# Two layernorms of a gated cross-attention block: applied by GpSimd in place of ScalarE

## The chip, the cores and the metric

One core of a Trainium2 chip. The metric is the device time of one execution in microseconds (us), the median over the runs. Engines by their names in the profile: PE and PEld are TensorE's matmuls and weight loads, DVE is VectorE, ACT is ScalarE, POOL is GpSimd, SP is SyncE.

## The reference

The input x is 16 tiles of 128 tokens by 256 features; each tile has a context of the same shape.

```python
def _layernorm(x, axis=-1, eps=1e-05):
    m = jnp.mean(x, axis=axis, keepdims=True)
    v = jnp.var(x, axis=axis, keepdims=True)
    return (x - m) / jnp.sqrt(v + eps)

x = x + jnp.tanh(g_xattn[0]) * _L0_xattn_ref(_layernorm(x, axis=-1), ctx_2048, Wq, Wk, Wv)
x = x + jnp.tanh(g_ffn[0]) * _L0_ffn_ref(_layernorm(x, axis=-1), wq_gate, s_gate, wq_up, s_up, wq_down, s_down)
```

`_L0_xattn_ref` is a cross-attention of 32 heads of width 8: queries from the first normalized x, keys and values from the context, an rms norm of each head's query and key, softmax, weighted sum. `_L0_ffn_ref` is a gated feed-forward layer of width 704 (silu of the gate times up, then down) on the second normalized x, with quantized integer weights. A layernorm ends as x times root plus offset, where root is 1/sqrt(v + eps) and offset is -m times root: one pair of numbers for each token, and a token is a partition.

## The kernel before

The 16 tiles go through in pairs. An iteration p (from -1 to 9) holds three stages of different tiles: it loads and projects the tiles 2p+2 and 2p+3, runs the attention of the tiles 2p-1 to 2p+1, and runs the feed-forward layer of pairs p-1 and p-2. Each engine has its own program, with the order of its work in an iteration written out by hand in a function `iteration(p)`; engines meet only at semaphores, and each engine works strictly in its order. `run` (line 302) unrolls the first iterations and the last ones and makes a hardware loop of p = 2 to 5. With e = 0 or 1 for the two halves of an iteration:

- TensorE (line 1420): `turn(p, e)` (line 1265) transposes the context and then the normalized tile `xn[:, e]` (L1273, L1277); it waits for `xn_ready`, count 2p+e+3, that is, for the first layernorm of tile 2p+e+2. `queries_keys(p, e)` (line 1290) and `values(p, e)` project (both L1286), `scores` (L1231) and `weigh` (L1250) are the attention, `out_rows` turns its result (L1319), `turn2(p)` (line 1341, L1351) transposes the second layernorm `x1n` of a pair, `chunk(p, j)` (L1371) are the six gate and up products and `down(p, e)` (L1396) the down product. Between the last matmul of `queries_keys(p, 0)` and `turn(p, 1)` TensorE has: scores, weigh, chunks 2 and 3, scores, weigh, chunk 4, weigh, scores, chunk 5.
- ScalarE (line 705): exponentials (L530), copies out of PSUM, squares of q and k (`square`, L572), tanh of the gate (L645), the upper part `h_hi` of the hidden values (`upper`, L656), and both layernorms: `normalize(p, e)` (line 585, L599) writes `xn[:, 1-e]` for tile b = 2p+e+3, and `normalize2(p, e)` (line 602, L611) writes `x1n[:, 1-e]` for tile b = 2p+e-1. So `turn(p, 1)` reads what `normalize(p, 0)` wrote, and `turn(p+1, 0)` reads what `normalize(p, 1)` wrote.
- VectorE (line 1104): statistics, the chain of small steps for the reciprocal roots (`roots`, L782 to L788; one chain serves the rms norms and the second layernorm), the upper half-precision part of q and k (`qk_upper`, L917), the copies that double it (`qk_double`, L929 to L931, after GpSimd's `split_qk`), the lower parts `xc_lo` (L894) and `x_lo` (L1028), the gates of the feed-forward layer (L983, L998). `up` of chunk j also waits until `h_lo` of chunk j-3 is done.
- GpSimd (line 477): in each iteration, in this order, `add_attention(p, 0)` (L443), `split_chunks` of chunks 0 and 1 (L434, the lower part `h_lo`), `qk_norm(p, 0)` (L466, q and k times their roots), `split_chunks` of chunk 2, `split_qk(p, 0)` (L426, the lower half-precision part), chunks 3, 4 and 5, `add_attention(p, 1)`, `qk_norm(p, 1)`, `split_qk(p, 1)`, and two `add_y` (L452, L454: scale and add the result of the feed-forward layer).

The roots of all 16 tiles for the first layernorm are made by VectorE in three batches early on (`x_bias_ready`), so `normalize` needs nothing new in the steady state. `normalize2` needs `x1_bias_ready`, which ends the root chain of the same half (`x1_offset`, L878).

Of the kernel before, what the change touches and what calls it, by code (L numbers as in the profile page):

```python
# [28 lines left out]
ALU = mybir.AluOpType  # L29
# [30 lines left out]
def build_program(nc, x, ctx, g_xattn, g_ffn, Wq, Wk, Wv, wq_gate, s_gate, wq_up, s_up, wq_down, s_down, out):  # L60
# [64 lines left out]
    with ExitStack() as stack:  # L125
# [188 lines left out]
        def has_tile(p, b):  # L314
            return 0 <= b < B if isinstance(p, int) else True
# [79 lines left out]
        @block.gpsimd  # L395
        def _(pool):
            nc.gpsimd.memset(ident[:], 0.0).then_inc(ident_zeroed, 1)
            pool.wait_ge(ident_zeroed, 1)
            nc.gpsimd.affine_select(out=ident[:], in_=ident[:], compare_op=ALU.not_equal, fill=1.0, base=0,
                                    pattern=[[-1, P]], channel_multiplier=1).then_inc(ident_ready, 1)  # L400

            nc.gpsimd.memset(v_blocks[:], 0.0).then_inc(v_zeroed, 1)
            pool.wait_ge(v_zeroed, 1)

            for e in range(2):
                v = v_blocks[:, e, 0:24 * BLOCK].rearrange("p (t c) -> p t c", c=3 * BLOCK)
                for i in range(3):
                    nc.gpsimd.memset(v[:, :, i * (BLOCK + SLOTW) + HD:i * (BLOCK + SLOTW) + HD + 1], 1.0)
                w = v_blocks[:, e, 24 * BLOCK:].rearrange("p (t c) -> p t c", c=2 * BLOCK)
                for i in range(2):  # L410
                    nc.gpsimd.memset(w[:, :, i * (BLOCK + SLOTW) + HD:i * (BLOCK + SLOTW) + HD + 1], 1.0)

                last = nc.gpsimd.memset(w[:, :, 3 * SLOTW - 1:3 * SLOTW], 1.0)
            last.then_inc(v_ready_ones, 1)

            nc.gpsimd.memset(y_sb[:, 0, :], 0.0).then_inc(result_ready, 1)
            nc.gpsimd.memset(y_sb[:, 1, :], 0.0).then_inc(result_ready, 1)

            def split_qk(p, e):

                b = 2 * p + e
                if not has_tile(p, b + 2):
                    return
                pool.wait_ge(qk_hi_ready, b + 3)
                pool.wait_ge(unit_ready, b + 3)
                nc.gpsimd.tensor_tensor(qk_parts[:, :, 1, :], qk_unit[:], qk_parts[:, :, 0, :],  # L426
                                        ALU.subtract).then_inc(qk_lo_ready, 1)

            def split_hidden(p, q, j):

                n = NJ * (p - q) + j
                pool.wait_ge(h_hi_ready, n + 1)
                r = rows(j)
                nc.gpsimd.tensor_tensor(h_lo[0:r, j, :], hidden[0:r, j % 3, :], h_hi[0:r, j, :].bitcast(F32),  # L434
                                        ALU.subtract).then_inc(h_lo_ready, 1)

            def add_attention(p, e):

                b = 2 * p + e - 1
                if has_tile(p, b):  # L440
                    k, n = use(p, f"out{e}")
                    pool.wait_ge(drained[k], n)
                    nc.gpsimd.tensor_tensor(tile_of(b), tile_of(b), attn[:], ALU.add).then_inc(x1_ready, 1)  # L443

            def add_y(p, e):

                if isinstance(p, int) and p == PAIRS + 1:
                    return
                done = 2 * (p - 2) + e
                k, n = use(p, f"y{e}")  # L450
                pool.wait_ge(drained[k], n)
                nc.gpsimd.tensor_tensor(y_sb[:, e, :], y_sb[:, e, :], down_scale[:], ALU.mult).then_inc(y_scaled, 1)  # L452
                pool.wait_ge(y_scaled, done + 1)
                nc.gpsimd.tensor_tensor(tile_of(done), tile_of(done), y_sb[:, e, :], ALU.add).then_inc(result_ready, 1)  # L454

            def qk_norm(p, e):

                b = 2 * p + e
                if not has_tile(p, b + 2):
                    return  # L460
                pool.wait_ge(root_steps, (ROOT_STEPS + 1) * (b + 3))
                k, m = use(p, f"qk{e}")
                pool.wait_ge(drained[k], m)
                if since(b, -1):
                    pool.wait_ge(qk_lo_ready, b + 2)
                nc.gpsimd.tensor_tensor(qk_unit[:], qk_raw[:], root_y[:, 0:2 * H].unsqueeze(2).to_broadcast([P, 2 * H, HD]),  # L466
                                        ALU.mult).then_inc(unit_ready, 1)

            def real(p, task):
                return here(p, task) and not (isinstance(p, int) and p == 0)  # L470

            def split_chunks(p, q, chunks):
                if real(p, f"ffn{chunks[0]}"):
                    for j in chunks:
                        split_hidden(p, q, j)

            def iteration(p):
                add_attention(p, 0)
                split_chunks(p - 1, 1, (0, 1))
                qk_norm(p, 0)  # L480
                split_chunks(p, 2, (2,))
                split_qk(p, 0)
                split_chunks(p, 2, (3, 4, 5))
                add_attention(p, 1)
                qk_norm(p, 1)
                split_qk(p, 1)
                if real(p, "y0"):
                    add_y(p, 0)
                    add_y(p, 1)

            run(pool, iteration)

        @block.scalar
        def _(act):
# [87 lines left out]
                        act.wait_ge(qk_hi_ready, b + 2)  # L582
                    nc.scalar.copy(qk_raw[:].rearrange("p h d -> p (h d)"), bank[k][:]).then_inc(drained[k], 1)

            def normalize(p, e):

                b = 2 * p + e + 3
                if not has_tile(p, b):
                    return
                if isinstance(b, int):  # L590
                    batch = 1 + [b < last for first, last in BATCHES].index(True)
                    act.wait_ge(x_bias_ready, batch)
                    one = slice(b, b + 1)
                else:
                    one = bass.ds(b, 1)
                if since(b, 2):
                    k, m = use(p, "turn0") if e else use(p - 1, "turn1")
                    act.wait_ge(filled[k], m)
                nc.scalar.activation(xn[:, 1 - e, :], tile_of(b), ACT.Identity, bias=x_bias[:, one],  # L599
                                     scale=x_root[1][:, one]).then_inc(xn_ready, 1)  # L600

            def normalize2(p, e):

                b = 2 * p + e - 1
                if not has_tile(p, b):
                    return
                act.wait_ge(x1_bias_ready, b + 1)
                if since(b, 2):
                    k, m = use(p if e else p - 1, "turn2")
                    act.wait_ge(filled[k], m)  # L610
                nc.scalar.activation(x1n[:, 1 - e, :], tile_of(b), ACT.Identity, bias=x1_bias[:], scale=root_y[:, 2 * H:]).then_inc(x1n_ready, 1)  # L611

            def drain_y(p, e):

                task = f"y{e}"
# [68 lines left out]
            def begin(p):  # L684
# [10 lines left out]

                exp_octet(p, 0, 1)
                drain_v(p, 0)
                if not first:
                    normalize(p, 0)
                upper(p - 1, 1, 0)  # L700
                if isinstance(p, int) and p == PAIRS + 1:
                    tanh_chunk(p, 2, 2)
# [2 lines left out]
            def iteration(p):  # L705
# [3 lines left out]

                exp_octet(p, 0, 2)  # L710
                copy_qk(p, 0)
                if first:
                    normalize(p, 0)
                if not (isinstance(p, int) and p == PAIRS + 1):
                    tanh_chunk(p, 2, 2)
                tanh_chunk(p, 2, 3)

                exp_octet(p, 0, 3)
                upper(p, 2, 2)
                if isinstance(p, int) and p == PAIRS - 1:  # L720
                    normalize2(p, 0)
                tanh_chunk(p, 2, 4)
                if ending(p):
                    upper(p, 2, 3)
# [1 line left out]
                drain_pv(p, 1)  # L726
                exp_octet(p, 1, 0)
                tanh_chunk(p, 2, 5)
                if isinstance(p, int) and p == PAIRS:
                    normalize2(p, 0)  # L730
                turn_hi(p, 1)

                exp_octet(p, 1, 1)
                if not ending(p):
                    upper(p, 2, 3)
                    normalize2(p, 0)
                upper(p, 2, 4)
                drain_v(p, 1)
                upper(p, 2, 5)
                if first:  # L740
                    convert_gate_up()
                    square(p, 1)
                    copy_qk(p, 1)
                    convert_down()
                    normalize(p, 1)
                else:
                    normalize(p, 1)
                    square(p, 1)
                    copy_qk(p, 1)

# [2 lines left out]
                drain_y(p, 0)  # L753

                exp_octet(p, 1, 3)
                if not (isinstance(p, int) and p == 0):
                    normalize2(p, 1)
                drain_y(p, 1)
                tanh_chunk(p, 1, 0)
                tanh_chunk(p, 1, 1)  # L760
                if isinstance(p, int) and p == 0:
                    normalize2(p, 1)
                begin(p + 1)

            upper_weight(0)
            normalize(-2, 1)
            upper_weight(1)
            begin(FIRST)
            run(act, iteration)
# [726 lines left out]
```

## Time and profile before

| | us |
|---|---|
| median of 3 runs | 257.71 |
| lowest, highest | 256.37, 260.33 |
| span of the profiled execution, first to last instruction | 254.6 |
| PE busy in the span | 217.0 (85%) |
| DVE busy | 189.1 (74%) |
| ACT busy | 176.9 (69%) |
| POOL busy | 107.6 (42%) |

The runs give whole device times; the profiled execution has only its span. The median of the runs is 3.1 us above that span, so a predicted span is compared with the runs after adding 3.1 us. A busy share says how much of the span an engine worked, not whether the end waited for it. Times in the rows are counted from the start of the span.

### The profile page before, as it was taken

The numbers are of one execution on the slowest core, as the hardware profiler recorded it, in microseconds if no ns is written. First come the engines' busy times: TensorE is split into PE (matmuls) and PEld (weight loads), VectorE is DVE, ScalarE is ACT, GpSimd is POOL, SyncE is SP. The second block draws the span as 40 slices with busy tenths as digits, with TensorE's granted clock in tenths as the row PEclk, the third lists the DMA queues.
The fourth block names the chain that finished last, engine by engine and source line by source line (L and its number), as shares of the span: only waits on it lengthen the run. The fifth ranks groups of instructions, "written<-read, shape, count | busy, mean of one in ns | idle before, by whom it ended". The sixth has DMA issues, their size and how long they took to land.

```text
span 254.6 us, 7326 instructions
## 1 busy us (share of the span) xinstructions
PE 217.0 (85%) x2592; PEld 175.6 (69%) x2592; DVE 189.1 (74%) x583; ACT 176.9 (69%) x338; POOL 107.6 (42%) x145
## 2 busy tenths in 40 slices
PE   1664878949869999999999999999999998983974
PEld 1553746727558888778878887888788776773873
DVE  4587999872878778786878687968796887667163
ACT  3358593746877896879688958895889588455261
POOL 5012303031314382737184728463835473454442
PEclk9999996777999999999999999999999999999799
DMA  6798631405061524141323223322315041000001
GB/s 176 220 351 209 72 58 21 86 5 107 0 106 35 71 23 86 36 108 33 70 47 97 42 61 61 83 56 51 76 50 64 21 82 48 21 24 0 21 21 41
DMA packets 45128, 18.08 MB, mean 71 GB/s; under 512 B 36401, under 2 KB 44849, under 8 KB 45105
## 3 DMA queue, kind: packets, MB, share of 16 engines
q1 hardware_dynamic: 45104, 17.77, 32.9%
q8 instruction: 14, 0.23, 0.4%
q14 instruction: 10, 0.07, 0.1%
HBM read 7.28 MB, written 2.10 MB: 37 GB/s over the span
## 4 chain that ended last, share of the span: by engine, by line
PE 62%; DVE 17%; issue 8%; ACT 7%; DMA 2%; POOL 2%; SPq 1%; DVEq 0%; ACTq 0%
PE bank L1371 16%; PE bank L1286 14%; PE pv_ps L1250 10%; PE bank L1396 9%; PE score_ps L1231 5%; DVE silu L983 2%; PE bank L1319 2%; ACT probs L530 2%; DVE hidden L998 2%; ACT tanh_g L645 2%; DMA w_raw<-L_xattn_Wv_dram 2%; DVE xc_lo L894 1%; PE bank L1277 1%; PE bank L1273 1%; PE bank L1351 1%
## 5 line engine op out<-in xcount | busy, mean ns | idle before, releaser
L530 ACT ACTIVATE probs<-score_ps 128x1024 f32<-128x1024 f32 x64 | 66.0, 1033 | 2.7 <-PE score_ps L1231 2.7
L466 POOL TENSOR_TENSOR qk_unit<-qk_raw,root_y 128x512 f32<-128x512 f32 x16 | 17.4, 1084 | 86.0 <-DVE root_y L788 86.0
L1371 PE MATMUL bank<-x_hi,gu_hi 128*128 128x256 f32 (+1 forms) x192 | 49.8, 296 | 4.0 <-DVE hidden L998 2.0
L1250 PE MATMUL pv_ps<-probs,v_blocks 128*32 128x128 f32 x1024 | 43.0, 287 | 6.3 <-issue 3.8
L1371 PE MATMUL bank<-x_lo,gu_hi 128*128 128x256 f32 (+1 forms) x192 | 47.1, 281 | 0.0
L434 POOL TENSOR_TENSOR h_lo<-hidden,h_hi 128x256 fp32r<-128x256 f32 (+1 forms) x48 | 36.7, 772 | 21.1 <-ACT h_hi L656 20.3
L1371 PEld LDWEIGHTS bank<-x_hi,gu_hi 128*128 128x128 f32 (+1 forms) x192 | 34.3, 179 | 8.8 <-issue 4.6
L1250 PEld LDWEIGHTS pv_ps<-probs,v_blocks 128*32 128x32 f32 x1024 | 25.1, 112 | 15.8 <-issue 6.6
L1286 PE MATMUL bank<-w_hi,xc_hi 128*128 128x256 f32 x96 | 31.7, 330 | 3.8 <-DVE xc_lo L894 3.8
L1371 PEld LDWEIGHTS bank<-x_lo,gu_hi 128*128 128x128 f32 (+1 forms) x192 | 34.5, 180 | 0.0
L645 ACT ACTIVATE tanh_g<-bank,half_gate 128x256 f32<-128x256 f32 (+1 forms) x48 | 22.7, 474 | 14.8 <-PE bank L1371 13.4
L983 DVE SCALAR_TENSOR_TENSOR silu<-tanh_g,bank 128x256 f32<-128x256 f32 (+1 forms) x48 | 19.9, 415 | 13.5 <-ACT tanh_g L645 13.4
L1231 PE MATMUL score_ps<-q_stack,k_stack 32*128 32x128 f16 x512 | 26.0, 223 | 4.5 <-DMA k_stack<-qk_parts 4.5
L1286 PE MATMUL bank<-w_hi,xc_lo 128*128 128x256 f32 x96 | 29.1, 303 | 0.0
L1286 PE MATMUL bank<-w_lo,xc_hi 128*128 128x256 f32 x96 | 29.1, 303 | 0.0
L1286 PEld LDWEIGHTS bank<-w_hi,xc_hi 128*128 128x128 f32 x96 | 20.4, 213 | 8.7 <-DVE xc_lo L894 5.1
L1231 PEld LDWEIGHTS score_ps<-q_stack,k_stack 32*128 32x128 f16 x512 | 14.8, 95 | 15.5 <-issue 7.9
L1396 PE MATMUL bank<-dn_hi,h_hi 128*128 128x256 f32 x84 | 25.2, 327 | 0.0
L998 DVE SCALAR_TENSOR_TENSOR hidden<-silu,scales,bank 128x256 f32<-128x256 f32 (+1 forms) x48 | 22.9, 478 | 2.4
L426 POOL TENSOR_TENSOR qk_parts<-qk_unit,qk_parts 128x512 f16<-128x512 f32 x16 | 18.6, 1162 | 8.8 <-DVE qk_parts L917 8.8
L1396 PE MATMUL bank<-dn_hi,h_lo 128*128 128x256 f32 x84 | 22.1, 290 | 0.0
L656 ACT CAST h_hi<-hidden 128x256 fp32r<-128x256 f32 (+1 forms) x48 | 18.7, 405 | 3.8 <-DVE hidden L998 3.6
(108 smaller groups left out, 438.0 us busy)
## 6 DMA issues: line engine op xcount, KB each, us to landing
ctx_sb<-ctx_dram SPq DMA_DIRECT2D x16, 128.0 KB, 2.6
out_dram<-x_all SPq DMA_DIRECT2D x16, 128.0 KB, 1.8
x_all<-x_dram SPq DMA_DIRECT2D x1, 1536.0 KB, 11.3
dn_int<-L_ffn_wq_down_dram SPq DMA_DIRECT2D x1, 704.0 KB, 7.6
gu_int<-L_ffn_wq_gate_dram SPq DMA_DIRECT2D x1, 640.0 KB, 4.6
gu_int<-L_ffn_wq_up_dram SPq DMA_DIRECT2D x1, 640.0 KB, 5.6
x_all<-x_dram SPq DMA_DIRECT2D x1, 384.0 KB, 4.5
w_raw<-L_xattn_Wq_dram SPq DMA_DIRECT2D x1, 256.0 KB, 2.7
```

The lines of the kernel that those rows point to most:

```text
L426: nc.gpsimd.tensor_tensor(qk_parts[:, :, 1, :], qk_unit[:], qk_parts[:, :, 0, :], ALU.subtract).then_inc(qk_lo_ready, 1)
L434: nc.gpsimd.tensor_tensor(h_lo[0:r, j, :], hidden[0:r, j % 3, :], h_hi[0:r, j, :].bitcast(F32), ALU.subtract).then_inc(h_lo_ready, 1)
L530: nc.scalar.activation(probs[:, t % 2, :], score_ps[t % 2][:].rearrange("p h n -> p (h n)"), ACT.Exp, scale=float(HD) ** 0.5 / UNIT ** 2). ...
L645: nc.scalar.activation(tanh_g[0:r, j % 2, :], bank[k][0:r, 0:TOK], ACT.Tanh, scale=half_gate[0:r, j:j + 1]).then_inc(tanh_g_ready, 1)
L656: nc.scalar.copy(h_hi[0:r, j, :], hidden[0:r, j % 3, :]).then_inc(h_hi_ready, 1)
L983: nc.vector.scalar_tensor_tensor(out=silu2[0:r, j % 2, :], in0=tanh_g[0:r, j % 2, :], scalar=1.0, in1=bank[k][0:r, 0:TOK], op0=ALU.add, op ...
L998: nc.vector.scalar_tensor_tensor(out=hidden[0:r, j % 3, :], in0=silu2[0:r, j % 2, :], scalar=scales[0:r, 2, j:j + 1], in1=bank[k][0:r, TOK ...
L1231: last = nc.tensor.matmul(score_ps[t % 2][:, s, :], k_stack[of, e, g, :], q_stack[of, e, g, :], start=True, stop=True, tile_position=(BLOC ...
L1250: last = nc.tensor.matmul(pv_ps[BLOCK * quadrant:BLOCK * (quadrant + 1), region * P:(region + 1) * P], v_blocks[:, e, h * BLOCK:(h + 1) * ...
L1286: last = nc.tensor.matmul(dst, a[:, tile, KC * source + c, :], w[:, c, column * D:(column + 1) * D], start=(n == 1), stop=(n == 3 * KC))
L1371: last = nc.tensor.matmul(bank[k][0:r, a * TOK:(a + 1) * TOK], w[:, j, a, c, 0:r], xx[:, c, :], start=(n == 1), stop=(n == (4 if wide_weig ...
L1396: last = nc.tensor.matmul(bank[k][:, 0:D], hh[0:r, j, e * P:(e + 1) * P], w[0:r, j, :], start=(n == 1), stop=(n == (4 if wide_weights else ...
```

## The change

`normalize` and `normalize2` leave ScalarE's program and are made by GpSimd as one `tensor_scalar` with two per-partition scalars (times root, plus offset). Their places in GpSimd's iteration are new, and GpSimd's program is unrolled over all iterations in place of `run`.

```diff
+            def normalize(p, e):
+                b = 2 * p + e + 3
+                if not has_tile(p, b):
+                    return
+                pool.wait_ge(x_bias_ready, 1 + [b < last for first, last in BATCHES].index(True))
+                if b >= 2:
+                    k, m = use(p, "turn0") if e else use(p - 1, "turn1")
+                    pool.wait_ge(filled[k], m)
+                nc.gpsimd.tensor_scalar(xn[:, 1 - e, :], x_all[:, b, :], x_root[1][:, b:b + 1], x_bias[:, b:b + 1],
+                                        ALU.mult, ALU.add).then_inc(xn_ready, 1)
+
+            def normalize2(p, e):
+                b = 2 * p + e - 1
+                if not has_tile(p, b):
+                    return
+                pool.wait_ge(x1_bias_ready, b + 1)
+                if b >= 2:
+                    k, m = use(p if e else p - 1, "turn2")
+                    pool.wait_ge(filled[k], m)
+                nc.gpsimd.tensor_scalar(x1n[:, 1 - e, :], x_all[:, b, :], root_y[:, 2 * H:], x1_bias[:],
+                                        ALU.mult, ALU.add).then_inc(x1n_ready, 1)
...
             def iteration(p):
                 add_attention(p, 0)
                 split_chunks(p - 1, 1, (0, 1))
+                if p == FIRST:
+                    normalize(p, 0)
                 qk_norm(p, 0)
+                normalize2(p, 0)
                 split_chunks(p, 2, (2,))
                 split_qk(p, 0)
+                if p != FIRST:
+                    normalize(p, 0)
                 split_chunks(p, 2, (3, 4, 5))
                 add_attention(p, 1)
                 qk_norm(p, 1)
+                normalize2(p, 1)
                 split_qk(p, 1)
+                normalize(p, 1)
                 if real(p, "y0"):
                     add_y(p, 0)
                     add_y(p, 1)
 
-            run(pool, iteration)
+            normalize(-2, 1)
+            for p in range(FIRST, PAIRS + 2):
+                iteration(p)
...
-                nc.scalar.activation(xn[:, 1 - e, :], tile_of(b), ACT.Identity, bias=x_bias[:, one],
-                                     scale=x_root[1][:, one]).then_inc(xn_ready, 1)
...
-                nc.scalar.activation(x1n[:, 1 - e, :], tile_of(b), ACT.Identity, bias=x1_bias[:], scale=root_y[:, 2 * H:]).then_inc(x1n_ready, 1)
```

All calls of the two functions in ScalarE's program go.

## Rows read from the trace of the kernel before

**Rows 1.** the page: span and busy time of each engine

```profile
span 254.6 us, 7326 instructions
...
PE 217.0 (85%) x2592; PEld 175.6 (69%) x2592; DVE 189.1 (74%) x583; ACT 176.9 (69%) x338; POOL 107.6 (42%) x145
```

**Rows 2.** the page: the chain that ended last, by engine

```profile
PE 62%; DVE 17%; issue 8%; ACT 7%; DMA 2%; POOL 2%; SPq 1%; DVEq 0%; ACTq 0%
```

**Rows 3.** busy us by engine in one stretch, then clock, DMA, GB/s

```profile
117.00:142.00 25.00, 24.70 (x327) 20.07 (x318) 19.85 (x58) 20.27 (x40) 13.56 (x16) 1.00 0.29 63
```

**Rows 4.** TensorE's waits: us in total, times, longest

```profile
PE bank L1286 <- DVE xc_lo L894: 3.8, 6, 1.5
```

**Rows 5.** timeline, PE: start us, us, line, what, idle before

```profile
128.84 0.38 PE L1277 MATMUL bank<-ident,xn 128*128 128x128 f32 x2
...
140.64 0.38 PE L1277 MATMUL bank<-ident,xn 128*128 128x128 f32 x2
```

**Rows 6.** groups by form, ACT: busy us, mean ns, idle before

```profile
L611 ACT ACTIVATE x1n<-x_all,x_bias,root_y 128x256 f32 x8 | 4.9, 607 | 4.5 <-DVE x_bias L878 4.5
L599 ACT ACTIVATE xn<-x_all,x_bias,x_root_y 128x256 f32 x8 | 4.8, 605 | 0.0
```

**Rows 7.** groups by form, POOL

```profile
L443 POOL TENSOR_TENSOR x_all<-x_all,attn 128x256 f32 x8 | 5.9, 735 | 4.7 <-DVE attn L957 4.7
...
L416 POOL MEMSET y_sb<- 128x256 f32 x1 | 0.3, 312 | 0.0
L399 POOL TENSOR_SCALAR_AFFINE_SELECT ident<-ident 128x128 f32<-128x128 f32 x1 | 0.3, 294 | 0.2 <-POOL ident L397 0.2
```

**Rows 8.** timeline, POOL, one steady iteration

```profile
125.45 1.08 POOL L466 TENSOR_TENSOR qk_unit<-qk_raw,root_y 128x512 f32<-128x512 f32 x1 [4.53 <-DVE root_y L788]
127.16 1.17 POOL L426 TENSOR_TENSOR qk_parts<-qk_unit,qk_parts 128x512 f16<-128x512 f32 x1 [0.62 <-DVE qk_parts L917]
...
138.29 1.10 POOL L466 TENSOR_TENSOR qk_unit<-qk_raw,root_y 128x512 f32<-128x512 f32 x1 [3.77 <-DVE root_y L788]
139.35 1.19 POOL L434 TENSOR_TENSOR h_lo<-hidden,h_hi 128x256 fp32r<-128x256 f32 x1
140.50 1.16 POOL L426 TENSOR_TENSOR qk_parts<-qk_unit,qk_parts 128x512 f16<-128x512 f32 x1
```

**Rows 9.** timeline, DVE, the same stretch

```profile
125.46 1.62 DVE L917 TENSOR_TENSOR qk_parts<-qk_raw,root_y 128x512 f16<-128x512 f32 x1
...
137.82 0.22 DVE L788 SCALAR_TENSOR_TENSOR root_y<-root_p,root_y 128x65 f32<-128x65 f32 x1
...
138.80 1.13 DVE L917 TENSOR_TENSOR qk_parts<-qk_raw,root_y 128x512 f16<-128x512 f32 x1
```

**Rows 10.** timeline, PE, the first iterations: transposes of xn

```profile
27.23 0.64 PE L1277 MATMUL bank<-ident,xn 128*128 128x128 f32 x2
...
40.23 0.40 PE L1277 MATMUL bank<-ident,xn 128*128 128x128 f32 x2
...
67.42 0.38 PE L1277 MATMUL bank<-ident,xn 128*128 128x128 f32 x2
```

**Rows 11.** timeline, POOL, the first iterations

```profile
27.25 1.16 POOL L426 TENSOR_TENSOR qk_parts<-qk_unit,qk_parts 128x512 f16<-128x512 f32 x1 [0.63 <-DVE qk_parts L917]
...
40.57 1.16 POOL L426 TENSOR_TENSOR qk_parts<-qk_unit,qk_parts 128x512 f16<-128x512 f32 x1 [1.90 <-DVE qk_parts L917]
...
69.00 1.17 POOL L426 TENSOR_TENSOR qk_parts<-qk_unit,qk_parts 128x512 f16<-128x512 f32 x1 [0.63 <-DVE qk_parts L917]
```

**Rows 12.** PE in stretches: busy us, granted clock, DMA, GB/s

```profile
36.90:40.30 3.40, 1.12 (x15) 1.00 0.00 0
40.30:47.20 6.90, 6.90 (x49) 0.51 0.49 87
...
234.90:238.30 3.40, 3.40 (x16) 0.52 0.00 0
```

**Rows 13.** timeline, DVE, near the end

```profile
231.76 0.63 DVE L788 SCALAR_TENSOR_TENSOR root_y<-root_p,root_y 128x65 f32<-128x65 f32 x1
```

More of the change, by code:

```diff
@@ L583, in copy_qk @@
                     nc.scalar.copy(qk_raw[:].rearrange("p h d -> p (h d)"), bank[k][:]).then_inc(drained[k], 1)
[L585 to L598, printed above, removed]
-                nc.scalar.activation(xn[:, 1 - e, :], tile_of(b), ACT.Identity, bias=x_bias[:, one],
-                                     scale=x_root[1][:, one]).then_inc(xn_ready, 1)
[L602 to L610, printed above, removed]
-                nc.scalar.activation(x1n[:, 1 - e, :], tile_of(b), ACT.Identity, bias=x1_bias[:], scale=root_y[:, 2 * H:]).then_inc(x1n_ready, 1)
             def drain_y(p, e):
@@ L697, in begin @@
                 drain_v(p, 0)
-                if not first:
-                    normalize(p, 0)
                 upper(p - 1, 1, 0)
@@ L711, in iteration @@
                 copy_qk(p, 0)
-                if first:
-                    normalize(p, 0)
                 if not (isinstance(p, int) and p == PAIRS + 1):
@@ L719, in iteration @@
                 upper(p, 2, 2)
-                if isinstance(p, int) and p == PAIRS - 1:
-                    normalize2(p, 0)
                 tanh_chunk(p, 2, 4)
@@ L728, in iteration @@
                 tanh_chunk(p, 2, 5)
-                if isinstance(p, int) and p == PAIRS:
-                    normalize2(p, 0)
                 turn_hi(p, 1)
@@ L735, in iteration @@
                     upper(p, 2, 3)
-                    normalize2(p, 0)
                 upper(p, 2, 4)
@@ L744, in iteration @@
                     convert_down()
-                    normalize(p, 1)
                 else:
-                    normalize(p, 1)
                     square(p, 1)
@@ L755, in iteration @@
                 exp_octet(p, 1, 3)
-                if not (isinstance(p, int) and p == 0):
-                    normalize2(p, 1)
                 drain_y(p, 1)
@@ L760, in iteration @@
                 tanh_chunk(p, 1, 1)
-                if isinstance(p, int) and p == 0:
-                    normalize2(p, 1)
                 begin(p + 1)
             upper_weight(0)
-            normalize(-2, 1)
             upper_weight(1)
```

## The prediction

> **What bounds the kernel now.** I read the page first: the span is 254.6 us, PE is busy for 85% of it, ACT for 69%, POOL for 42% [rows 1]. Busy shares are averages, so next comes the chain that ended last: 62% of it is PE, 7% ACT [rows 2]. Then one steady stretch of 25 us, which is one iteration: PE is busy for 24.7 of 25.0 us, ACT for 20.3, POOL for 13.6 [rows 3]. So in the steady state TensorE is the bound, and no engine that is relieved can give back more than some 0.3 us an iteration; TensorE's own waits say the same, the nearest steady one being six waits on VectorE's `xc_lo` [rows 4]. Of the two layernorms on ScalarE no wait of TensorE in the steady state is seen. ScalarE spends 32 x 0.605 = 19.4 us on them (16 tiles, two norms; each of the two rows shown has a twin of 8) [rows 6], but it has nearly 5 us idle an iteration already.
>
> The question is then not what ScalarE gains but when the results are ready on GpSimd. The timelines of one iteration on PE, POOL and DVE answer that.
>
> **The price of one layernorm on GpSimd.** The trace has no such instruction, so bounds: below, GpSimd's write-only memset of 128x256, 0.31 us; above, `split_qk`, a two-input operation of twice the width, 1.16 us [rows 7, 8]. Nearer: a one-input operation of half the width takes 0.29 us, the two-input one of the same width 0.735 us [rows 7]. With 0.1 us fixed, the one-input row doubled gives about 0.49. There are two scalars to fetch, so I take 0.60, between 0.49 and 0.735, and 0.56 from start to start for back-to-back instructions.
>
> The Trainium skill (GPSIMD Engine Reference, section 3.1) gives 1.8 cycles an element at 1.2 GHz as the best case of its loops: by that an estimate of 0.38 us before dispatch. No row here shows it; by it alone the sum below would be about 5 us less.
>
> **The first layernorm for `turn(p, 1)`: the main cost.** `turn(p, 1)` transposes what `normalize(p, 0)` wrote. In the trace TensorE does that at 140.64 [rows 5]; ScalarE had the tile ready 8 us earlier. In the new order `normalize(p, 0)` stands behind `qk_norm(p, 0)`, `normalize2(p, 0)`, chunk 2's `h_lo` and `split_qk(p, 0)`. `qk_norm(p, 0)` can't start before the roots of the same iteration are done: the last root step starts at 137.82 and ends at 138.04, `qk_norm` starts at 138.29 [rows 8, 9]. Before, `split_qk` ended at 140.50 + 1.16 = 141.66, already 1.0 us after TensorE wants the tile. `normalize2` ahead of it adds 0.56, `normalize` itself 0.56, the semaphore 0.05: ready at 142.83. TensorE stands still for 142.83 - 140.64 = 2.2 us. All that TensorE has queued waits with it: scores, `out_rows`, weigh, `values`, `queries_keys(p, 1)`, `turn2`, `down`. Nothing of it gives the time back, because the next such chain starts only at the next `queries_keys(p+1, 0)`. Iterations 2 to 6 pay it: 5 x 2.2 = 11.0 us.
>
> The port between VectorE and GpSimd is in these numbers: `qk_upper` takes 1.13 us when it starts 0.59 us before GpSimd's `qk_norm` ends, and 1.62 us when it starts with it; each time it ends about 0.54 us after `qk_norm` does [rows 8, 9]. So the GpSimd instruction behind `qk_norm` waits 0.5 us in its turn (chunk 2 took 1.19 us). Before the change chunk 2 carried that wait, after it `normalize2` does; it is paid once either way.
>
> The Trainium skill (SBUF — State Buffer, "Who interferes with whom") says that a VectorE instruction with two SBUF inputs and a GpSimd instruction that reads block each other wholly, whoever comes second; these two durations agree. By a rule of shared bandwidth the sum would be the same to 0.2 us an iteration.
>
> **The first layernorm for `turn(p+1, 0)`.** `qk_norm(p, 1)` ended at 126.53, `qk_upper` at 127.08. `normalize2(p, 1)` starts behind `qk_norm`, is held until 127.08 and ends at 127.5 (0.16 of its 0.60 being start-up), `split_qk` ends at 128.66, `normalize(p, 1)` at 129.25, seen by TensorE at 129.30; it wanted the tile at 128.84 [rows 5, 8, 9]. That is 0.45 us, in iterations 1 to 5: 2.3 us. The two `add_y` behind it come some 0.9 us later, which GpSimd's idle time before the next `qk_norm` (3.77 us, [rows 8]) hides.
>
> **First iterations.** The layernorm of tile 1 is made as soon as its offset is there, as before, 0.1 us later by GpSimd's slower wake-up. `turn(0, 0)` was at 27.23; `normalize(-1, 1)` now follows a `split_qk` that ends at 28.41, so ready at 29.05: 1.8 us late, of which I take 1.4, since the following stretch hangs on VectorE (bounds 0 and 1.8). `turn(0, 1)` was at 40.23, the `split_qk` ends at 41.73, so 42.34: 2.1 us. `turn(1, 1)` was at 67.42; `split_qk` ended at 70.17, with `normalize2` ahead 70.5, ready at 71.1: 3.6 us, since this iteration has few chunks between projection and turn [rows 10, 11]. Together 7.2 us. The tile for `turn(1, 0)` has time to spare.
>
> **The end.** The last `normalize2` now blocks GpSimd until its roots are there, so the `h_lo` instructions no longer collide with VectorE's root steps: a step that took 0.63 us [rows 13] takes 0.22 elsewhere [rows 9], and one more is alike. That gives back 0.9 us, of which 0.4 goes again as `h_lo` of chunk 2 comes late for `up` of chunk 5. With an earlier `x_lo`, I take -0.7, bounds -1.0 and +0.5. Unrolling GpSimd's program I cost at nothing: its instructions start back to back in the loop already.
>
> **The clock.** In the stretch 36.9 to 40.3 PE was busy for only 1.12 us; then the granted clock is 0.51 for 6.9 us, that is the 1.2 GHz level, and after 234.9, behind a long idle stretch, 0.52 for 3.4 us [rows 12]. A stall of 2.2 us with light work about it comes near the first case. One such fall costs 3.4/2 = 1.7 us to 6.9/2 = 3.4 us. I take two falls (iteration 1, with its long stall, and one of the five others) at 2.5 us: 5 us. Bounds: none, and one for every stall.
>
> **Sum.** 254.6 + 11.0 + 2.3 + 0.1 + 7.2 - 0.7 + 5 = 279.5 us of span, 282.6 as a run (+3.1). I say 282.
>
> **Rivals.**
> 1. The same waits, the clock never falls: 282 - 5 = 277. For it: the steady stretch is at 1.00 throughout, and a stall is only a twelfth of an iteration. Chance 0.20.
> 2. The clock falls after nearly every stall: seven falls at 2.5 us in place of two, 277 + 17.5 = 295. For it: the fall after 40.3, behind an idle time of about the same length. Against: next to these stalls there are dense products, there were few. Chance 0.12. The Trainium skill (TensorE: Matmul & The Clock Gate, "HAM oscillation") describes kernels in which TensorE's wait in each turn of a loop brings the lower clock each time; the two falls here agree that idle time is what brings it.
> 3. GpSimd's layernorm costs as much as its slowest rows, 1.1 us in place of 0.6. Each such 0.1 us counts about 25 times 0.1 (two in each of the waits above, one in the first ones): +12.5, 290 with the clock as forecast. Against: it has one input. Chance 0.08. At 0.31 us the waits of `turn(p+1, 0)` vanish and the sum is about 7 us less, 275; that lies in the forecast's own range.
> 4. Not slower. The place is the path from `queries_keys(p, 0)` to `split_qk(p, 0)` on ScalarE and VectorE: if ScalarE without its 1.2 us a half iteration ran squares and tanh so much earlier that the roots came 2.2 us sooner, the tile would be there in time, and only the 0.3 us waits and the end would be left: 257.7 - 6 x 0.3 - 0.7 = 255. It decides from 2.2 us. Against: the root steps run back to back on VectorE, and ScalarE took the squares as soon as TensorE was done. Chance 0.10, most of it for a dependency that I read wrongly.
>
> **Chances.** Forecast 0.50, its own range 272 to 291; rivals 0.20, 0.12, 0.08, 0.10. The range 266 to 296 takes in rivals 1 to 3 and a cheap layernorm without a fall of the clock. Less than 2% is about what a measurement of this kernel can't tell from no change, that is 252.6 to 262.9: slower by more 0.90, within it 0.06, faster 0.04.
>
> **What would show it.** Right: TensorE waits at L1277 for GpSimd's `xn` in nearly every iteration, about 2.2 us for e = 1 and under 0.7 for e = 0; the period grows from 25.0 to 27.7 us; the layernorm takes near 0.6 us; ScalarE's busy time falls by 19 us and the time still rises; stretches at the 1.2 GHz level stand behind some of the stalls. Wrong: no wait at L1277; a layernorm over 1 us; the growth in VectorE's copies (a port that both want) in place of TensorE's wait; or a period that is unchanged.

## The result and the profile after

| | before | after |
|---|---|---|
| median, us | 258.94 (4 runs) | 285.62 (4 runs, 284.9 to 287.41) |
| span of the profiled execution, us | 254.6 | 283.3 |
| PE busy, us | 217.0 | 231.4 |
| mean granted clock of the profiled execution | 0.966 | 0.886 |

The ratio is 1.1116, 95% interval 1.1025 to 1.1207: the change makes the kernel 11% slower. (The median of before is over one run more than in the first table.) Ratios and intervals, here and below, leave out the runs in which the same kernel was in a slower state and use its other runs alone, so they are not the quotients of the medians in the table.

The page of the changed kernel, busy time by engine and the chain that ended last:

```profile
span 283.3 us, 7217 instructions
...
PE 231.4 (82%) x2592; PEld 185.4 (65%) x2592; DVE 185.8 (66%) x583; ACT 163.2 (58%) x306; POOL 128.0 (45%) x177
...
PE 54%; issue 15%; POOL 12%; DVE 11%; ACT 4%; DMA 1%; SPq 1%; DVEq 0%; ACTq 0%; POOLq 0%
```

Against [rows 1, 2]: ACT works 13.7 us less and POOL 20.4 us more, with 32 instructions moved. The forecast had 19.4 us for ACT, which is 32 durations added up [rows 6]; but in the trace of before these instructions overlap their neighbours (the layernorm at 132.13 lasts 0.60 us, the next instruction starts at 132.63), and busy time counts an overlap once. PE works 14.4 us more on the same 2592 matmuls, and it is idle for 283.3 - 231.4 = 51.9 us in place of 37.6. So the 28.7 us of the span are two nearly equal halves: 14.3 us in which TensorE waits, and 14.4 us in which the same work takes longer. Not all of the 14.4 is the change's: this execution also has a stretch at the lower clock from about 19 to 35 us, which the trace of before hasn't, and two kernels below without the late tile whose executions have it too show PE busy for 218.3 and 218.8 us, 1.3 to 1.8 above before. By stages (from one transpose of `xn` to another): 12.3 of the 28.7 us are lost by `turn(2, 1)` (102.80 in place of 90.50), 15.5 in the four steady iterations behind it, 0.9 after the last turn. POOL has risen in the chain from 2% to 12%. Lines of the code have moved: L1277 (transposes of `xn`) is now L1266, L1286 is L1275, L466 is L490, L426 is L450, and the two layernorms are L428 and L440.

Who TensorE waited for (us in total, times, longest):

```profile
PE bank L1266 <- POOL xn L428: 18.9, 10, 3.5
...
PE bank L1275 <- DVE xc_lo L883: 3.3, 2, 1.8
PE bank L1340 <- DVE hidden L987: 3.2, 1, 3.2
...
PE bank L1360 <- DVE x_lo L1017: 1.2, 1, 1.2
```

The first line is new and is the largest of all: 18.9 us in ten waits for GpSimd's first layernorm. Of the others that on `xc_lo` is a little smaller, in two waits where [rows 4] had six, that for the last turn is 3.2 us in place of 3.8, that on `x_lo` 1.2 in place of 2.0; none is more than 0.5 us larger than before.

GpSimd in one iteration, and the price of the layernorm by groups (busy us, mean ns):

```profile
126.53 1.08 POOL L490 TENSOR_TENSOR qk_unit<-qk_raw,root_y 128x512 f32<-128x512 f32 x1 [3.66 <-DVE root_y L777]
127.73 0.56 POOL L440 TENSOR_SCALAR x1n<-x_all,root_y,x_bias 128x256 f32<-128x256 f32 x1
128.25 1.16 POOL L458 TENSOR_TENSOR h_lo<-hidden,h_hi 128x256 fp32r<-128x256 f32 x1
129.38 1.15 POOL L450 TENSOR_TENSOR qk_parts<-qk_unit,qk_parts 128x512 f16<-128x512 f32 x1
130.51 0.55 POOL L428 TENSOR_SCALAR xn<-x_all,x_root_y,x_bias 128x256 f32<-128x256 f32 x1
...
142.69 1.07 POOL L490 TENSOR_TENSOR qk_unit<-qk_raw,root_y 128x512 f32<-128x512 f32 x1 [4.49 <-DVE root_y L777]
143.75 0.99 POOL L440 TENSOR_SCALAR x1n<-x_all,root_y,x_bias 128x256 f32<-128x256 f32 x1
144.71 1.17 POOL L450 TENSOR_TENSOR qk_parts<-qk_unit,qk_parts 128x512 f16<-128x512 f32 x1
145.86 0.56 POOL L428 TENSOR_SCALAR xn<-x_all,x_root_y,x_bias 128x256 f32<-128x256 f32 x1
```

```profile
L440 POOL TENSOR_SCALAR x1n<-x_all,root_y,x_bias 128x256 f32<-128x256 f32 x16 | 12.4, 773 | 9.9 <-DVE x_bias L867 9.3
...
L428 POOL TENSOR_SCALAR xn<-x_all,x_root_y,x_bias 128x256 f32<-128x256 f32 x16 | 9.3, 582 | 10.5 <-DVE x_bias L810 10.5
```

The order is the one written out in the change, and it answers to [rows 8]: `qk_norm` at 126.53, then `normalize2`, chunk 2, `split_qk`, and only at 130.51 the layernorm that TensorE needs. It takes 0.55 us and ends at 131.06. The group of `x1n` has a mean of 0.77 us since in the second half of an iteration it is held (0.99 us at 143.75, where VectorE's `qk_upper` runs from 142.85 to 144.32), and in the first half it isn't (0.56 us at 127.73, ahead of `qk_upper` at 127.94).

TensorE at the same places, and the granted clock about the stall (columns of the second fence: stretch, length, PE busy, instructions, clock, DMA, GB/s):

```profile
102.80 0.44 PE L1266 MATMUL bank<-ident,xn 128*128 128x128 f32 x2 [1.90 <-POOL xn L428]
...
131.12 0.69 PE L1266 MATMUL bank<-ident,xn 128*128 128x128 f32 x2 [1.91 <-POOL xn L428]
...
147.18 0.38 PE L1266 MATMUL bank<-ident,xn 128*128 128x128 f32 x2
...
160.69 0.44 PE L1266 MATMUL bank<-ident,xn 128*128 128x128 f32 x2 [1.92 <-POOL xn L428]
...
188.86 0.69 PE L1266 MATMUL bank<-ident,xn 128*128 128x128 f32 x2 [1.92 <-POOL xn L428]
...
218.50 0.44 PE L1266 MATMUL bank<-ident,xn 128*128 128x128 f32 x2 [1.83 <-POOL xn L428]
```

```profile
97.50:101.00 3.50, 3.41 (x46) 1.00 0.00 0
101.00:104.50 3.50, 1.70 (x17) 0.85 0.00 0
104.50:108.00 3.50, 3.50 (x32) 0.66 0.96 75
108.00:111.50 3.50, 3.50 (x44) 1.00 0.55 119
...
129.00:132.50 3.50, 1.59 (x13) 0.75 0.00 0
132.50:136.00 3.50, 3.50 (x28) 0.50 0.35 67
136.00:139.50 3.50, 3.50 (x40) 0.77 0.56 121
139.50:143.00 3.50, 3.50 (x43) 1.00 0.00 0
```

Each of the turns with e = 1 waits 1.8 to 1.9 us [rows 5: no idle time there before]; the turn with e = 0 at 147.18 doesn't wait. After each stall the clock is at its 1.2 GHz level for a while, about 3.3 us behind the stall at 102.80 and about 6.5 us behind the one at 131.12; the iterations are alternately 28.3 and 29.6 us long (102.80, 131.12, 160.69, 188.86, 218.50), against 25.0 before.

### The profile page after: what moved, and what is told of

Read it like the earlier page. It is cut to its first block, busy times and chain, and to the rows that moved or that the text cites. A ratio compares the mean times of both kernels' runs of the same rounds, so it can differ in the third digit from the quotient of the medians.

```text
span 283.3 us, 7217 instructions
## 1 busy us (share of the span) xinstructions
PE 231.4 (82%) x2592; PEld 185.4 (65%) x2592; DVE 185.8 (66%) x583; ACT 163.2 (58%) x306; POOL 128.0 (45%) x177
## 4 chain that ended last, share of the span: by engine, by line
PE 54%; issue 15%; POOL 12%; DVE 11%; ACT 4%; DMA 1%; SPq 1%; DVEq 0%; ACTq 0%; POOLq 0%
PE bank L1275 15%; PE bank L1385 10%; PE pv_ps L1239 8%; PE bank L1360 7%; PE score_ps L1220 5%; POOL qk_parts L450 4%; POOL qk_unit L490 3%; PE bank L1308 3%; PE bank L1266 2%; POOL xn L428 2%; POOL h_lo L458 2%; ACT probs L563 2%; DMA w_raw<-L_xattn_Wv_dram 1%; PE bank L1340 1%; DVE hidden L987 1%
## 5 line engine op out<-in xcount | busy, mean ns | idle before, releaser
L490 POOL TENSOR_TENSOR qk_unit<-qk_raw,root_y 128x512 f32<-128x512 f32 x16 | 17.2, 1076 | 77.2 <-DVE root_y L777 77.2
L1239 PE MATMUL pv_ps<-probs,v_blocks 128*32 128x128 f32 x1024 | 45.3, 299 | 6.8 <-issue 4.3
L1275 PE MATMUL bank<-w_hi,xc_hi 128*128 128x256 f32 x96 | 35.6, 371 | 3.4 <-DVE xc_lo L883 3.3
L1239 PEld LDWEIGHTS pv_ps<-probs,v_blocks 128*32 128x32 f32 x1024 | 26.1, 116 | 17.0 <-issue 8.0
L650 ACT ACTIVATE tanh_g<-bank,half_gate 128x256 f32<-128x256 f32 (+1 forms) x48 | 22.7, 473 | 19.9 <-PE bank L1360 17.8
L1275 PE MATMUL bank<-w_lo,xc_hi 128*128 128x256 f32 x96 | 32.4, 337 | 0.0
L1275 PE MATMUL bank<-w_hi,xc_lo 128*128 128x256 f32 x96 | 32.1, 334 | 0.0
L972 DVE SCALAR_TENSOR_TENSOR silu<-tanh_g,bank 128x256 f32<-128x256 f32 (+1 forms) x48 | 19.9, 414 | 16.0 <-ACT tanh_g L650 15.9
L1275 PEld LDWEIGHTS bank<-w_hi,xc_hi 128*128 128x128 f32 x96 | 24.3, 254 | 8.9 <-issue 4.6
L956 DVE BATCH_NORM_STATS2 x_stats<-x_all 128x6 f32<-128x256 f32 (+1 forms) x16 | 6.8, 427 | 27.5 <-POOL x_all L467 27.5
L1275 PEld LDWEIGHTS bank<-w_lo,xc_hi 128*128 128x128 f32 x96 | 24.4, 254 | 0.0
L1275 PEld LDWEIGHTS bank<-w_hi,xc_lo 128*128 128x128 f32 x96 | 23.8, 248 | 0.0
```

The source lines that it names most:

```text
L650: nc.scalar.activation(tanh_g[0:r, j % 2, :], bank[k][0:r, 0:TOK], ACT.Tanh, scale=half_gate[0:r, j:j + 1]).then_inc(tanh_g_ready, 1)
L972: nc.vector.scalar_tensor_tensor(out=silu2[0:r, j % 2, :], in0=tanh_g[0:r, j % 2, :], scalar=1.0, in1=bank[k][0:r, 0:TOK], op0=ALU.add, op ...
L1239: last = nc.tensor.matmul(pv_ps[BLOCK * quadrant:BLOCK * (quadrant + 1), region * P:(region + 1) * P], v_blocks[:, e, h * BLOCK:(h + 1) * ...
L1275: last = nc.tensor.matmul(dst, a[:, tile, KC * source + c, :], w[:, c, column * D:(column + 1) * D], start=(n == 1), stop=(n == 3 * KC))
```

## The experiments

Theory: the time is lost at one place, `turn(p, 1)`, since `normalize(p, 0)` stands behind `split_qk(p, 0)` in GpSimd's order; a direct wait and the lower clock that each wait brings. Rival: it is the load, 32 more instructions on an engine that shares a port with VectorE. The median of before, over the runs that the ratios use, was 258.35 us for the first four experiments, 258.59 us for the next three and 258.84 us for the last two (over all runs 259.32, 259.22 and 259.23 us). The recorded ratios and the quotients of these medians differ by up to 0.005, so a difference of half a per cent is settled by neither.

**One layernorm in another place.**

```diff
-                if p == FIRST:
-                    normalize(p, 0)
+                normalize(p, 0)
                 qk_norm(p, 0)
...
                 split_qk(p, 0)
-                if p != FIRST:
-                    normalize(p, 0)
```

> Both layernorms stay on GpSimd, only normalize(p, 0) moves ahead of qk_norm(p, 0). Place theory (TensorE waits because that layernorm stands behind split_qk): the e=1 waits at the xn transposes, 1.9 us in each steady iteration and 3.5 us in iteration 1, go, and with them the stretches at the 1.2 GHz level behind them; TensorE's wait on xn falls from 18.9 us to 2 to 4 us (the first turns and e=0), the period from 28.9 to about 25.5 us, the time to 258 to 264 us. Load theory (GpSimd's longer program and the port that it shares with VectorE cost the time): the time stays above 275 us, since the same 32 instructions run on the same engine.

Measured: 258.26 us, ratio 1.0013 (0.9974 to 1.0052). Its waits and a steady stretch (busy us of PE, PEld, DVE, ACT, POOL, then clock):

```profile
PE bank L1263 <- POOL xn L428: 3.1, 2, 1.7
```

```profile
117.00:142.00 25.00, 24.91 (x325) 20.14 (x325) 19.95 (x59) 18.59 (x36) 16.33 (x21) 1.00 0.29 63
```

The wait for `xn` is 3.1 us in two, both in the first iterations. The steady clock is 1.00, the period 24.8 us. POOL is busy for 16.3 of 25 us where it had 13.6 [rows 3], and this costs nothing: the load theory falls here. The move of one call gives back the whole loss, 27 us.

**The other half early too.** In addition, `normalize(p, 1)` ahead of `qk_norm(p, 1)`:

```diff
+                normalize(p, 1)
                 qk_norm(p, 1)
                 normalize2(p, 1)
                 split_qk(p, 1)
-                normalize(p, 1)
```

> As the run before, and normalize(p, 1) ahead of qk_norm(p, 1) too, so no first layernorm stands behind a split_qk. Place theory: no wait on xn is left but that of tile 1 (1.2 us, there before as well); the time is that of the kernel before within 1%, or a little below by the end (255 to 260 us). Load theory: no better than the run before, above 275 us.

Measured: 258.82 us, ratio 0.9991 (0.9945 to 1.0036). Left is one wait of 2.6 us for `xn`, that of tile 1, which a kernel with ScalarE's layernorm shows at 2.6 us too in one of its executions (the unrolled kernel below). Nothing more is gained by it than by the first move; the steady period is 25.0 us.

**Is it the clock?** The changed kernel, with TensorE given something to do where it stands still:

```diff
                 k = claim(p, f"turn{e}")
+                if e == 1 and since(p, 2):
+                    for _ in range(14):
+                        nc.tensor.matmul(bank[k][:, 0:D], dn_hi[:, 0, 0:P], dn_hi[:, 0, :], start=True, stop=True)
                 pe.wait_ge(ctx_loaded[e], 16 * (p + 2))
```

> The changed kernel, with 14 extra matmuls of 128x256 (about 1.7 us at 2.4 GHz, their result overwritten) put into TensorE's stall ahead of turn(p, 1) for p of 2 and more. They fill a wait of 1.9 us. Clock theory (half of the lost time is the lower clock that each stall brings): the clock stays at the 2.4 GHz level in the steady state, mean granted clock 0.94 or more against 0.886, period near 27.2 us, time 8 to 11 us below the changed kernel, 274 to 278 us, though TensorE does more. Wait theory (the stalls alone cost, the low clock is hidden by other waits): the time stays within 2 us of 285.6 or rises.

Measured: 277.12 us, ratio 1.0678 (1.0614 to 1.0742); that is 8.5 us below the changed kernel, with 70 matmuls more. Two stretches of it and its wait (PE busy, instructions, clock):

```profile
120.00:148.00 28.00, 27.73 (x344) 1.00 0.30 64
148.00:176.00 28.00, 27.70 (x361) 1.00 0.30 64
```

```profile
PE bank L1269 <- POOL xn L428: 10.8, 10, 3.5
```

With the stall filled the clock stays at 1.00 in the steady state and the iteration takes 26.8 us. (The profiled execution is the fastest of the four, with a mean clock of 0.947; the other three, without a trace of their own, have 0.907 to 0.913 and are 1.2 to 2.0 us longer.) The order of GpSimd is the same and the tile is as late as before (0.3 us of wait are left beside the filling). So of the 3.9 us that an iteration of the changed kernel is longer (28.9 on the mean against 25.0), 1.8 are the late tile and 2.1 are the lower clock that the standstill brings. The wait theory (stalls alone) falls.

**Unrolling alone.** The kernel before with one edit:

```diff
-            run(pool, iteration)
+            for p in range(FIRST, PAIRS + 2):
+                iteration(p)
```

> The kernel before with nothing changed but GpSimd's program unrolled. No layernorm is moved. Theory that unrolling is free: ratio 1.00 within 0.5%. Rival: in the changed kernel qk_norm starts 0.17 us sooner after the last root step and takes the port ahead of the one-column offset (0.93 us in place of 0.15), which puts qk_upper 0.4 us later in each half (p, 0); by it this run shows the same 0.9 us offset instruction in the steady iterations, and the time is 0 to 2 us above before, more likely near 0 as TensorE does not wait there.

Measured: 258.02 us, ratio 0.9939 (0.9899 to 0.9979), a little faster, where I had expected nothing or a loss. The medians are nearer to each other, 258.02 against 258.35 us, 0.999, so the size of the gain isn't settled. The offset instruction does take 0.92 us, as the rival says (VectorE and GpSimd in the first half of an iteration):

```profile
140.18 0.22 DVE L789 SCALAR_TENSOR_TENSOR root_y<-root_p,root_y 128x65 f32<-128x65 f32 x1
...
140.65 0.92 DVE L879 SCALAR_TENSOR_TENSOR x_bias<-x_mean_var,root_y 128x1 f32<-128x1 f32 x1
...
141.89 0.91 DVE L918 TENSOR_TENSOR qk_parts<-qk_raw,root_y 128x512 f16<-128x512 f32 x1
```

```profile
140.48 1.08 POOL L466 TENSOR_TENSOR qk_unit<-qk_raw,root_y 128x512 f32<-128x512 f32 x1 [3.20 <-DVE root_y L789]
```

`qk_norm` now starts 0.30 us after the last root step's start, before 0.47 [rows 8, 9], and starts ahead of the offset, which then ends with it. The time isn't longer for it. What the trace shows as gained is at another place, where VectorE's copies meet GpSimd's two `add_y`:

```profile
132.06 0.38 DVE L930 COPY qk_parts<-qk_parts 128x256 f32<-128x256 f32 x1
132.37 0.75 DVE L931 COPY qk_parts<-qk_parts 128x128 f32<-128x128 f32 x1
133.04 0.21 DVE L932 COPY qk_parts<-qk_parts 128x128 f32<-128x128 f32 x1
...
133.46 0.62 DVE L895 TENSOR_TENSOR xc_lo<-bank,xc_hi 128x512 fp32r<-128x512 f32 x1
```

```profile
130.75 0.73 POOL L452 TENSOR_TENSOR y_sb<-y_sb,down_scale 128x256 f32<-128x256 f32 x1
131.56 0.73 POOL L454 TENSOR_TENSOR x_all<-x_all,y_sb 128x256 f32<-128x256 f32 x1
132.25 0.78 POOL L452 TENSOR_TENSOR y_sb<-y_sb,down_scale 128x256 f32<-128x256 f32 x1
```

GpSimd's instructions follow each other 0.81 us apart where the loop had 0.92 (128.28 and 129.20 in the trace of before), so the copies (L930 to L932) meet other gaps: 0.38, 0.75 and 0.21 us, against 0.77, 0.75 and 0.21 before. `xc_lo` comes earlier, the 0.3 us wait that TensorE had for it in each steady iteration is gone (two such waits are left, where [rows 4] had six), and the period is 24.8 us. That is some 1.2 us over five iterations. It is a matter of which instructions happen to meet, not of unrolling as such: the run with both halves early and that with the second layernorm alone (below) are unrolled too, and keep six such waits and 25.0 us.

**One norm at a time.** First the first layernorm alone on GpSimd, in its places of the change (the calls of `normalize2` stay in ScalarE's program, those of `normalize` go):

> Only the first layernorm moves to GpSimd, in the places of the change; the second stays on ScalarE. Place theory: the tile for turn(p, 1) still stands behind split_qk, but without the 0.56 us of normalize2 ahead of it: steady wait at the xn transposes 1.9 - 0.56 = 1.3 us in place of 1.9, and the lower clock behind at least some of the stalls; time 268 to 280 us. Load theory: half the load, so half of the 27 us: 272 us, with the growth spread and no wait at the xn transposes that explains it.

Measured: 279.53 us, ratio 1.0846 (1.0764 to 1.0928). The steady wait is 1.5 us (1.3 expected): `normalize2` ahead of it is worth 0.4 us of lateness, and the rest of the chain alone is enough for the stall.

```profile
PE bank L1301 <- POOL xn L428: 16.4, 10, 3.2
```

Then the second layernorm alone on GpSimd, the first on ScalarE:

> Only the second layernorm moves to GpSimd, in the places of the change; the first stays on ScalarE. Place theory: nothing of TensorE's waits for it in the steady state, so 256 to 261 us, ratio within 1% of before, by 0 to 1 us better at the end. Load theory: half the load, half the loss, 272 us.

Measured: 258.85 us, ratio 0.9992 (0.9937 to 1.0047). The same count of instructions moved costs 20 us in the one case and nothing in the other, so it isn't the load.

**How early is early enough?** Both on GpSimd, `normalize(p, 0)` right behind `qk_norm(p, 0)`:

```diff
                 qk_norm(p, 0)
+                if p != FIRST:
+                    normalize(p, 0)
                 normalize2(p, 0)
...
                 split_qk(p, 0)
-                if p != FIRST:
-                    normalize(p, 0)
```

> Both on GpSimd, normalize(p, 0) right behind qk_norm(p, 0), ahead of normalize2, chunk 2 and split_qk. It tests the sum of the chain: the last root step ends, qk_norm ends some 1.4 us later, the layernorm takes 0.55 us (0.5 more if it is held by the port), so the tile is ready 2.0 to 2.5 us after the last root step, and TensorE wants it 2.6 us after. Place theory: no steady wait or one under 0.2 us, 258 to 263 us. Rival (anything behind qk_norm is too late, as TensorE needs the tile before the roots are done): waits of 1 us or more, 268 us and up.

Measured: 263.57 us, ratio 1.0193 (1.0113 to 1.0272), at the upper edge of what was expected. GpSimd and TensorE in the steady state:

```profile
121.38 1.08 POOL L490 TENSOR_TENSOR qk_unit<-qk_raw,root_y 128x512 f32<-128x512 f32 x1 [3.61 <-DVE root_y L777]
122.44 0.56 POOL L428 TENSOR_SCALAR xn<-x_all,x_root_y,x_bias 128x256 f32<-128x256 f32 x1
```

```profile
123.90 0.38 PE L1266 MATMUL bank<-ident,xn 128*128 128x128 f32 x2
```

The tile is ready at 123.00 and TensorE takes it at 123.90, without a wait: 0.9 us to spare, and the period is 24.7 us. What is left of the loss is in the first iterations, which have fewer chunks between projection and turn: four waits, 7.2 us in all. One of them is tile 1's, 2.6 us in this execution as in two others that lose nothing by it; the other three (1.7, 1.8 and 1.1 us) make 4.6. My expectation had left these out.

**Does a version beat both?** The version with `normalize(p, 0)` early, and `normalize(-1, 1)` early as well:

> The version with normalize(p, 0) early, and normalize(-1, 1) early too, so that no turn of the first iterations waits for a split_qk either. Place theory: against the version with normalize(p, 0) early the 1.7 us wait at the xn transposes of turn(0, 0) goes; of it 0.5 to 1.4 us are saved; ratio to before 0.990 to 0.998. Rival (the first iterations hang on VectorE and the clock, not on that wait): no difference from the version with normalize(p, 0) early, ratio 0.996 to 1.003.

Measured: 258.13 us, ratio 0.993 (0.9902 to 0.9959). The wait at `turn(0, 0)` is gone; of the waits for `xn` only tile 1's is left, 1.2 us. By the interval it is the first version with both layernorms on GpSimd that is faster than the kernel before, by 0.7%; by the medians (258.13 against 258.84 us) it is 0.3%, and the version without this last move has 258.26 us. So neither a gain over the kernel before nor one over that version is settled, and its interval overlaps that of the plain unrolled kernel: that the layernorms' move brings any gain isn't shown.

The kernel before, unrolled, with only the three last second layernorms on GpSimd:

> The kernel before with GpSimd's program unrolled, and of the layernorms only the last three second ones (p of 7 and 8) on GpSimd. In the last iterations the two steps of VectorE's root chain that GpSimd's h_lo held up should run at 0.22 us, TensorE's longest wait for the last turn2 falls from 3.8 to 3.2 us, and the steady state keeps the period of the unrolled kernel, 24.8 us. Expected ratio 0.988 to 0.994, below the unrolled kernel by 0.5 us. Rival (the saved 0.6 us goes again on the last chunks): same as the unrolled kernel, 0.994.

Measured: 257.51 us, ratio 0.9963 (0.992 to 1.0005). TensorE's longest wait for the last turn is 3.2 us in place of 3.8, as expected, but the ratio lies above the expected 0.988 to 0.994 and is not told apart from the unrolled kernel's or from 1. In the profiled executions the part behind the last transpose of `xn` takes 64.8 us here and 64.9 us in the unrolled kernel, so the 0.6 us don't show in the time, as the rival said. Inconclusive.

## Why the prediction was right

282 us was forecast, 285.62 measured. In spans, where the sum was made, it is 279.5 against 283.3 us, or 24.9 us more against 28.7 (between its span and its run the profiled execution of after has 2.1 us, not the 3.1 that were added). The place and its cause are right and shown. That the number came so near is in part luck, since two terms are off in opposite directions: TensorE's idle time grew by 14.3 us where the sum has 19.9, and its work by 14.4 us where the sum has 5. By step:

- **What bounds the kernel.** Right. ScalarE's relief (13.7 us of busy time, not the 19.4 of the forecast) brings nothing by itself; with the place mended, the kernel is where it was.
- **The price of one layernorm.** 0.60 us forecast, 0.55 us measured undisturbed, and the spacing 0.52 us for 0.56.
- **The tile for `turn(p, 1)`.** Right in place and cause, shown by moving the one call. 2.2 us forecast, 1.9 us measured: the layernorms were 0.04 us cheaper each, and `qk_norm` started 0.17 us sooner after the root step in the unrolled program. Who carries the hold by the port was told wrongly: `normalize2` got the port ahead of `qk_upper`, and chunk 2 was held as before (1.16 us). The sum didn't depend on it.
- **The tile for `turn(p+1, 0)`.** 0.45 us in five iterations forecast. In the steady iterations no wait for it is listed in the changed kernel; at 117.69 the transposes of `xn` start 0.42 us behind those of the context where 0.28 is usual, so 0.14 us at most, and in every second iteration TensorE comes well behind the tile (at 147.18 it is ready since 146.42). The wait of `turn(2, 0)`, 1.10 us at 89.50, I had not seen at all. This step of the sum, 2.3 us, measured about 1.4 (1.10 and twice 0.14).
- **First iterations.** 1.8, 2.1 and 3.6 us late forecast, 1.71, 1.94 and 3.46 us of wait measured (of the 1.8 the sum took only 1.4). The 0.1 us for tile 1 isn't there: TensorE waits 1.19 us for it, before 1.23. The three waits, and that of `turn(2, 0)`:

```profile
29.17 0.69 PE L1266 MATMUL bank<-ident,xn 128*128 128x128 f32 x2 [1.71 <-POOL xn L428]
...
44.01 0.44 PE L1266 MATMUL bank<-ident,xn 128*128 128x128 f32 x2 [1.94 <-POOL xn L428]
...
74.92 0.69 PE L1266 MATMUL bank<-ident,xn 128*128 128x128 f32 x2 [3.46 <-POOL xn L428]
...
89.50 0.44 PE L1266 MATMUL bank<-ident,xn 128*128 128x128 f32 x2 [1.10 <-POOL xn L428]
```

- **The end.** The wait before the last turn is 3.2 us in place of 3.8, so 0.6 of the forecast 0.7 us are there as a wait. The part behind the last turn of a tile is 0.9 us longer all the same, since the clock fell behind the stall at 218.50: TensorE waits 1.3 us less in it and works 2.2 us longer.
- **The clock.** This is the term that was mis-sized: "I take two falls ... 5 us". The clock falls at seven of the stalls, those that end at 44.01 (1.94 us) and 74.92 (3.46 us) and the five of 1.8 to 1.9 us; the fall at 44.01 stands for the one that before had at 40.3 [rows 12], so six are new. It doesn't fall at the stall of 1.10 us at 89.50. TensorE's work takes 14.4 us longer in all, of which some 1.5 are the low stretch near the start. The filled stall shows 8.5 us of the time to hang on the clock, at least, as it fills only five of the stalls. This is the mechanism of rival 2, seven falls, to which 0.12 was given; its 295 us are too high, since the stalls are shorter than in the sum and a fall costs 2.1 us of the iteration, not 2.5. The iteration is 28.9 us long on the mean, 27.7 forecast. What made up for it is that TensorE's idle time grew less than the waits for `xn`: these are 17.7 us more than before (20.6 in the sum), and other waits shrank by 3.4 us, where the sum has 0.7.
- **The port.** Right as to the hold: `normalize2` takes 0.99 us where it starts behind `qk_upper` and 0.56 us where it starts ahead of it.
- **Unrolling at nothing.** Near enough: the unrolled kernel is faster by 0.3 us (medians) to 1.6 us (ratio 0.9939), and the steady iterations of the trace give 1.2.

The Trainium skill (TensorE: Matmul & The Clock Gate, "HAM oscillation") describes a loop in which each turn's wait, there a longer one for a DMA, throws TensorE back to its lower clock. The runs here agree: 1.9 us of standstill in each iteration was enough in the changed kernel, and filling it kept the clock at 1.00.

## What to carry to other kernels

When work moves to an engine with a fixed order, its price is its place: write down when its consumer wants it, and what the instructions ahead of it in the new order themselves wait for. Here 32 instructions on another engine cost nothing, and one call behind a chain that ends too late cost 27 us. A stall of TensorE of 1.9 us in each iteration counted double here (3.9 us), since the clock fell with it; harmless matmuls in five such stalls gave back 8.5 of the 27 us.

## What was not expected of the hardware

- A short standstill is enough: 1.9 us idle, with transposes and small matmuls about it, and the granted clock fell behind each of the five steady stalls, for about 3.3 or 6.5 us in turn. In the trace of before 2.3 us without work between 36.9 and 40.3 had done it once [rows 12].
- Extra work made it faster: 14 matmuls of 128x256 in each of five stalls, 8.5 us less.
- Unrolling the program on GpSimd moved its instructions by 0.1 to 0.2 us, enough to change which of two instructions started first: a one-column instruction of VectorE that now starts behind GpSimd's `qk_norm` took 0.92 us in place of 0.15 and ended with it (at 141.57 and 141.56), at no cost to the time, while the doubling copies took less and the period fell from 25.0 to 24.8 us.
- Executions of one kernel, that with `normalize(p, 0)` early, had mean granted clocks from 0.926 to 0.966 and times from 257.3 to 260.7 us, which is as much as the smaller differences above, and the times don't follow the clocks (257.3 us at 0.966, 257.4 at 0.926); what decides it wasn't tried.
